# Linear attention on one core: query and key features over three PSUM banks, the next turn's first values product ahead of the state's update, the row transposes beside the key transposes, the scores in one run

## What is computed

```
B, S, D, H, DH = 4, 1024, 256, 16, 64          # all in float32
h = _ln(_layernorm(x), g1, beta1)
q = elu((h @ wq) per head @ proj) + 1
k = elu((h @ wk) per head @ proj) + 1
v = (h @ wv) per head
def step(carry, qkv_t):                         # over the S positions
    kv = kv + k_t[..., :, None] * v_t[..., None, :]
    ksum = ksum + k_t
    num = einsum('bhd,bhde->bhe', q_t, kv)
    den = einsum('bhd,bhd->bh', q_t, ksum) + 1e-06
    return (kv, ksum), num / den
attn = outs.reshape(b, s, H * DH) @ wo
x = normalised x + attn
```

## Time and profile before

| | us |
|---|---|
| median of 3 runs | 3779.68 (3776.72 to 3782.56) |
| the profiled execution, its own time | 3780.14 |
| its span, first to last instruction | 3778.3 |
| the stage of linear attention, about | 1214 to 2036 of the span |
| one turn of it, of 32 | 25.8 |
| TensorE busy, of the span | 3591.0 (95%) |
| mean granted TensorE clock | 0.989 |

### The profile page before, as it was taken

One profiled execution on the slowest core, in us unless ns is written; L12 is line 12 of the kernel. 1 busy time (PEld: TensorE's weight loads), 2 busy tenths in 40 slices (PEclk: granted clock), 3 DMA queues, 4 the chain that ended last, 5 costly groups with the idle time before them and its releaser, 6 DMA issues. The chain is left out here.

```text
span 3778.3 us, 59344 instructions
## 1 busy us (share of the span) xinstructions
PE 3591.0 (95%) x21704; PEld 2545.8 (67%) x21704; DVE 2510.6 (66%) x5351; ACT 1605.8 (42%) x3142; POOL 1403.5 (37%) x1569
## 2 busy tenths in 40 slices
PE   7889888887999999999999998999999999999999
PEld 5666666665556888888886665666656566666565
DVE  8999999997665555555554546777743367777432
ACT  5878777773001222222222214666631156666211
POOL 6988888885000000000001223444421134444111
PEclk9999999999999999999999999999999999999999
DMA  1000000002101000001001211111111111121121
GB/s 41 1 12 12 12 12 12 2 6 87 39 32 42 12 9 13 11 11 35 11 11 55 74 58 61 39 34 57 35 60 51 36 60 35 35 72 34 45 67 39
DMA packets 150758, 129.33 MB, mean 34 GB/s; under 512 B 20852, under 2 KB 147592, under 8 KB 150472
## 3 DMA queue, kind: packets, MB, share of 16 engines
q1 hardware_dynamic: 150472, 125.54, 10.7%
HBM read 87.73 MB, written 37.77 MB: 33 GB/s over the span
## 5 line engine op out<-in xcount | busy, mean ns | idle before, releaser
L420 POOL TENSOR_TENSOR ssm_acc<-ssm_acc,ssm_weighted 128x512 f32<-128x512 f32 x255 | 337.7, 1333 | 103.6 <-ACT ssm_weighted L565 103.0
L406 POOL TENSOR_SCALAR ssm_ub<-ssm_uT,ssm_bcT 128x512 f32<-128x512 f32 x512 | 357.5, 717 | 25.2 <-PE ssm_pu L1107 21.4
L1107 PEld LDWEIGHTS ssm_pu<-ident,ssm_ub 128*128 128x128 f32 x2048 | 239.6, 143 | 183.9 <-issue 87.5
L1107 PE MATMUL ssm_pu<-ident,ssm_ub 128*128 128x128 f32 x2048 | 310.2, 280 | 50.4 <-DVE ssm_state L780 33.1
L3074 PE MATMUL win_pa<-win_w_wqkv,tile_hT 128*128 128x512 f32 x744 | 342.7, 597 | 0.0
L1123 PE MATMUL ssm_pt<-ident,ssm_state 128*128 128x128 f32 x2040 | 278.8, 278 | 48.2 <-DVE ssm_acc L790 30.2
L2507 PE MATMUL glu_up<-block_hT,glu_w_w 128*128 128x512 f32 x704 | 310.0, 599 | 8.0 <-DVEq L82 8.0
L780 DVE TENSOR_TENSOR_SCAN ssm_state<-ssm_da,ssm_carry,ssm_pu 128x512 f32<-128x512 f32 x256 | 312.6, 1263 | 3.0 <-ACT ssm_da L553 3.0
L2845 POOL TENSOR_TENSOR block_hT<-tile_straight,tile_turned 128x512 f32<-128x512 f32 x124 | 157.9, 1274 | 401.9 <-DVE tile_turned L2952 401.7
L780 DVE TENSOR_TENSOR_SCAN ssm_state<-ssm_da,ssm_pu 128x512 f32<-128x512 f32 x256 | 297.0, 1202 | 5.4 <-PE ssm_pu L1107 2.7
L2889 ACT ACTIVATE win_probs<-win_sc,win_nbias,tile_rn 128x256 f32<-128x256 f32 x512 | 281.9, 560 | 28.7 <-DVE win_nbias L2980 21.8
(11 more groups left out here) (368 smaller groups left out, 7475.1 us busy)
## 6 DMA issues: line engine op xcount, KB each, us to landing
x<-block_y SPq DMA_DIRECT2D x16, 512.0 KB, 2.9
block_add<-x SPq DMA_DIRECT2D x16, 512.0 KB, 5.6
tile_raw<-in_tables SPq DMA_DIRECT2D x64, 128.0 KB, 2.2
a<-tile_y SPq DMA_DIRECT2D x64, 128.0 KB, 1.7
block_xs<-a SPq DMA_DIRECT2D x32, 256.0 KB, 3.3
block_x<-a SPq DMA_DIRECT2D x16, 512.0 KB, 5.2
x<-block_half_y SPq DMA_DIRECT2D x16, 256.0 KB, 2.1
block_x<-x SPq DMA_DIRECT2D x8, 512.0 KB, 3.9
```

Of the source, the lines that this page charges most:

```text
L406: nc.gpsimd.tensor_scalar(ub[:, i % 2, t, :], uT[:, k % 2, t, :], bcT[:, k % 2, t, n:n + 1], 1.0, ALU.mult, ALU.mult).then_inc(ub_ready.se ...
L420: nc.gpsimd.tensor_tensor(acc[:, k % 2, t, :], acc[:, k % 2, t, :], weighted[:, j, :], ALU.add)\
L1107: last = nc.tensor.transpose(pu[c][:, t * P:(t + 1) * P], ub[:, i % 2, t, c * P:(c + 1) * P], ident)
```

## The change

Four edits, all in `linear_attention_stage`; no product, copy or transfer is added or removed.

- The four groups of queries and keys go to `pa[0]`, `pa[1]`, `pc[2]`, `pa[0]` (`feature_banks`). Group 2 waits for the state's update of the turn before last instead of group 0's features, group 3 waits for group 0's features. In turn, the numerators' third bank `pc[2]` waits until VectorE has read group 2. The values go to `pa[1]` and `pa[0]` (`value_banks`), and wait for the features that read those.
- `values(turn.next(), 0)` stands between the numerators and the products for the state (L2069 in the changed file), not behind the latter.
- `transposes(turn.next())` stands right behind the key transposes, ahead of both halves of the scores, which so follow each other.
- On ScalarE the two `k_rows` copies stand ahead of the copy of `h`.

```diff
+        feature_banks, value_banks = [pa[0], pa[1], pc[2], pa[0]], [pa[1], pa[0]]
...
-                    nc.scalar.activation(grown[:, g % 2, :], pa[g % 2][:, :], ACT.Exp).then_inc(exp_ready.sem, 1)
+                    nc.scalar.activation(grown[:, g % 2, :], feature_banks[g][:, :], ACT.Exp).then_inc(exp_ready.sem, 1)
...
             def body(turn, before, more, more2):
 
+                act.wait_ge(keep_in.sems[turn.side], keep_in.at(turn))
+                for g in range(2):
+                    act.wait_ge(kt_ready.sem, kt_ready.at(turn.i, g + 1))
+
+                    nc.scalar.activation(
+                        k_rows[:, g * GP:(g + 1) * GP, :], pb[g][:, :].rearrange("p (r d) -> p r d", d=P), ACT.Copy,
+                        scale=keep[:, turn.side, :]).then_inc(k_rows_ready.sem, 1)
                 act.wait_ge(h_ready.sem, h_ready.at(turn.i))
                 act.wait_ge(y_ready.sem, y_ready.at(turn.i - 1))
                 nc.scalar.activation(h_keep[:, :], h[:, turn.side, :], ACT.Copy).then_inc(kept.sem, 1)
-                act.wait_ge(keep_in.sems[turn.side], keep_in.at(turn))
-                for g in range(2):
-                    act.wait_ge(kt_ready.sem, kt_ready.at(turn.i, g + 1))
...
                 for g in range(4):
                     if g < 2:
-                        pe.wait_ge(v_ready.sem, v_ready.at(turn.i - 1, g + 1))
+                        pe.wait_ge(v_ready.sem, v_ready.at(turn.i - 1, 2 - g))
+                    elif g == 2:
+                        pe.wait_ge(state_ready.sem, state_ready.at(turn.i - 2, 3))
                     else:
-                        pe.wait_ge(phi_ready.sem, phi_ready.at(turn.i, g - 1))
+                        pe.wait_ge(phi_ready.sem, phi_ready.at(turn.i, 1))
...
             def values(turn, g):
-                pe.wait_ge(phi_ready.sem, phi_ready.at(turn.i, 3 + g))
+                pe.wait_ge(phi_ready.sem, phi_ready.at(turn.i, 2 + 2 * g))
...
-                scores_of(turn, 1)
                 if more:
                     transposes(turn.next())
+                scores_of(turn, 1)
                 scores_of(turn, 0)
...
                     pe.wait_ge(state_ready.sem, state_ready.at(i - 1, c + 1))
+                    if c == 2 and more:
+                        pe.wait_ge(phi_ready.sem, phi_ready.at(i + 1, 3))
...
+                if more:
+                    values(turn.next(), 0)
                 pe.wait_ge(k_rows_ready.sem, k_rows_ready.at(i))
...
-                if more:
-                    values(turn.next(), 0)
                 pe.wait_ge(attn_ready.sem, attn_ready.at(i))
```

More of the change, by code:

```diff
@@ L1857, in values @@
                 nc.scalar.activation(v[:, turn.side, g * heads:(g + 1) * heads, 0:DH],
-                                                pa[g][:, :].rearrange("p (h d) -> p h d", d=DH), ACT.Copy).then_inc(v_ready.sem, 1)
+                                                value_banks[g][:, :].rearrange("p (h d) -> p h d", d=DH), ACT.Copy).then_inc(v_ready.sem, 1)
             def body(turn, before, more, more2):
-                act.wait_ge(h_ready.sem, h_ready.at(turn.i))
-                act.wait_ge(y_ready.sem, y_ready.at(turn.i - 1))
-                nc.scalar.activation(h_keep[:, :], h[:, turn.side, :], ACT.Copy).then_inc(kept.sem, 1)
                 act.wait_ge(keep_in.sems[turn.side], keep_in.at(turn))
@@ L1871, in body @@
                         scale=keep[:, turn.side, :]).then_inc(k_rows_ready.sem, 1)
+                act.wait_ge(h_ready.sem, h_ready.at(turn.i))
+                act.wait_ge(y_ready.sem, y_ready.at(turn.i - 1))
+                nc.scalar.activation(h_keep[:, :], h[:, turn.side, :], ACT.Copy).then_inc(kept.sem, 1)
                 if more:
@@ L1916, in features @@
                         qkT[:, turn.side, g // 2, g % 2 * GP:(g % 2 + 1) * GP, :],
-                        pa[g % 2][:, :].rearrange("p (r t) -> p r t", t=P), 0.0,
+                        feature_banks[g][:, :].rearrange("p (r t) -> p r t", t=P), 0.0,
                         grown[:, g % 2, :].rearrange("p (r t) -> p r t", t=P), ALU.max, ALU.add).then_inc(phi_ready.sem, 1)
@@ L1997, in queries_keys @@
                         for k in range(KD):
-                            last = nc.tensor.matmul(pa[g % 2][:, r * P:(r + 1) * P], wqk[:, g // 2, k, cols],
+                            last = nc.tensor.matmul(feature_banks[g][:, r * P:(r + 1) * P], wqk[:, g // 2, k, cols],
                                                     hT[:, k, :], start=(k == 0), stop=(k == KD - 1))
@@ L2002, in values @@
             def values(turn, g):
-                pe.wait_ge(phi_ready.sem, phi_ready.at(turn.i, 3 + g))
+                pe.wait_ge(phi_ready.sem, phi_ready.at(turn.i, 2 + 2 * g))
                 for k in range(KD):
-                    last = nc.tensor.matmul(pa[g][:, :], hT[:, k, :], wv[:, k, g * 512:(g + 1) * 512],
+                    last = nc.tensor.matmul(value_banks[g][:, :], hT[:, k, :], wv[:, k, g * 512:(g + 1) * 512],
                                             start=(k == 0), stop=(k == KD - 1))
```

## The result

| | before | after |
|---|---|---|
| median, us (4 runs each) | 3778.26 (3776.72 to 3782.56) | 3745.35 (3739.96 to 3746.80) |
| ratio, 95% interval | | 0.9908 (0.9891 to 0.9926) |
| the profiled execution, us | 3780.14 | 3739.96 |
| first key transpose of the stage, us of the span | 1214.47 | 1208.93 |
| that to the next stage's first product, us | 824.46 | 792.40 |

The forecast was 3745.6 for the median. "Before" has one run more here than in the table ahead of the prediction. The profiled execution of the changed kernel is the fastest of its four, and 40.2 us under that of before. Of these, 32.1 us lie in the stage; 5.5 us lie ahead of it, where the two programs are the same, and 2.6 behind it.

A forecast was written before the change was run, and what follows sets the result against it. TensorE was taken to bound the stage; 0.41 + 0.36 + 0.35 - 0.03 = 1.09 us a turn, 34.1 us in all, gave a median of 3745.6 us. Range 3739 to 3756, with 3739 to 3749 at 0.70.

The forecast's parts named there:

- scores in one run, copies of keys first: Head of a turn: one excursion into 64-row halves instead of two, and no late k_rows; 0.41 us a turn.
- residual as a wait: Row transposes, moved ahead, would wait for VectorE's residual to read pt; costs 0.03 us a turn, between 0 and 0.25.
- third bank: Queries and keys: group 2 no longer waits for group 0's features, so the weight loads run on; 0.36 us a turn.
- values ahead: Values product ahead of the state's products hides the wait for the division, 0.30, plus 0.05 from neighbours; 0.35 us a turn.
- The head: From the first key transpose to the first query product: 3.18 to 3.21 us instead of 3.59.
- the margin of 0.2 us for the copies: Both k_rows copies end near 1631.87; the second half of the scores wants pb at about 1632.17, weights 0.1 earlier.
- better neighbours: Values ahead: 64-column products left for transposes rather than 512-column products lose 0.05 instead of 0.10 us; 0.05 won.
- The entry into 64 columns: State's products behind a 512-column values product: the mode change costs 0 to 0.09 us, taken as 0.09; hidden gives 3742.7.
- Only the visible idle: Rival: only the idle shown returns, 0.69 us a turn, 21.4 us in all, giving 3758 us; chance of 3753 to 3761: 0.07.
- The residual in earnest: Rival: the residual wait costs 0.08 to 0.25 us a turn, 3747 to 3752.5 us; chance 0.16 together with k_rows still late.
- The third bank or the copies do nothing: Rival: another wait ends in the same place, say k_rows still late, 3752 us; chance 0.16 shared with the residual rival.
- Slower: Rival: the later state update outgrows its 4.2 us margin around the turn; 3789 us at 5.6 us longer; chance 0.04.

The follow-up runs named there:

- split: Changed kernel with the row transposes put back between the two halves of the scores, copies of the keys still first: 25.124 us a turn, median 3756.52 us.
- run with fourteen statistics: Changed kernel with fourteen extra, unused VectorE statistics of h ahead of n: 25.92 us a turn, one run of 3782.31 us.
- the two comparisons: Changed kernel against the kernel before, measured twice: 3745.35 against 3778.26 us (ratio 0.9908), then with no edit 3742.49 against 3777.33 us (0.9905).
- the first three: Changed kernel with one part undone each: third bank 3753.97 us, first values behind the state's products 3755.96, row transposes between the score halves 3756.52.

## Why the prediction was right, step by step

| per turn, us | forecast | in the changed kernel's starts | undone alone |
|---|---|---|---|
| scores in one run, copies of keys first | 0.41 | 0.38 | split 0.32; copies 0.38 |
| residual as a wait | -0.03 | 0 | |
| third bank | 0.36 | 0.35 | 0.352 |
| values ahead | 0.35 | 0.29 | 0.287 |
| sum | 1.09 | 1.02 | |

**The head.** Forecast 3.18 to 3.21 us, measured 3.20; the gain is 0.38 where I had 0.41. The missing 0.03 is the wait for `k_rows`. It didn't go, it shrank from 0.06 to 0.03. In the changed kernel the copies end at 1608.82 + 1.27 = 1610.09 and the weights of the second half of the scores start at 1610.20, the same 0.11 later as wherever they waited. No idle shows, since TensorE still runs the products of the first half, but the loads behind come late. The run with fourteen statistics shows the price, since its scores start after the copies are done:

```profile
1658.57 1.16 PE L2026 MATMUL lin_pc<-lin_space 64*128 64x128 f32 x16
1659.57 1.06 PE L2026 MATMUL lin_pb<-lin_space 64*128 64x128 f32 x16
1660.56 0.71 PE L2004 MATMUL lin_pa<-lin_hT,lin_wqk 128*128 128x128 f32 x4
```

From the first score to the first query it takes 1.99 us there and 1611.33 - 1609.31 = 2.02 in the changed kernel. What failed is the margin of 0.2 us for the copies. I let the first of them start the moment the fourth transpose ends, 0.60 after the first, and it starts 0.10 later; and I didn't take off the 0.11 from the end of a copy to the weights that wait for it, which I used for the residual. Together they eat the margin. So the second excursion was worth 0.35, as forecast, and the copies 0.03 instead of 0.06.

**The residual as a wait.** The weights of the row transposes start at 1608.92, 0.12 after the residual's end at 1608.80, so they are held for about 0.03 us, where I had 0.02. But the product doesn't need them yet: it starts at 1609.00, 0.11 after the last key transpose. That costs nothing where I had 0.03. So this error and that of the head cancel.

**The third bank.** Right: 0.352 against 0.36, with group 3's weights at 1616.68, 1.5 us after group 0's features (1615.20). Neither the numerators' third bank nor the values wait for the features.

**The values.** This term was mis-sized. The wait for the division was put at 0.30 and is 0.29. The 0.05 for better neighbours is zero. I had compared the run behind the state's products, 1.98 for the values against 1.88 (0.10) with 1.09 for the transposes against 1.04 (0.05). What I left out is that the values have a new neighbour too: behind the numerators' 65-column products their run takes 1.93, 0.05 longer than 1.88. The move spares 0.10 there and pays 0.05 twice. The entry into 64 columns behind a 512-column product was the unknown, between 0 and 0.09: its first product comes 0.52 after the last of the values (with 0.43 the step of those), so this cost is there in full. The other reading was that weight loads are pulled ahead of products in flight, as the Trainium skill, "TensorE: Matmul & The Clock Gate", part 2, says for row groups that don't conflict. This trace doesn't show it at this change of mode: the first weights of the state's products start at 1625.74, together with their own product.

**The sum.** A turn of 24.80 us lies outside the 24.7 to 24.75 that I named as a sign: 0.06 are missing at the values, and the two 0.03 cancel. The other signs came as said (row transposes 0.11 behind, no idle among the loads of queries and keys, 0.52 ahead of the state's products). Thirty turns at 1.02 are 30.7 us, where I had 32.7; the last one gave 0.30, as forecast, and turn 0 gave 0.92, where I had 1.1. Turn 0 depends on the clock too, which is 0.91 there in both traces (in the run with ScalarE's old order turn 0 takes 26.46 us at 0.94, in the changed kernel 27.13). With small change that makes 32.1 us, where I had 34.1. That the median came within 0.3 us of the forecast is partly luck: the base was 3779.7 then, and with more runs it is 3777 to 3779; and a launch scatters by more than the 2 us that the sum was off. By the medians of the two comparisons the gain is 32.9 and 34.8 us, each uncertain by some 6.

**The undone parts add up.** 0.352 + 0.287 + 0.320 + 0.06 for the copies in the old order is 1.02 us, the whole. The stage is 11.0, 8.9 and 9.5 us longer in the traces of the first three than in that of the changed kernel, where 31 turns give 10.9, 8.9 and 9.9. By launch times they lie 11.5, 13.5 and 14.0 us over the changed one's 3742.5 on that chip, up to 5 us more, while launches of the changed kernel alone lie up to 13 us apart.

**The rivals.** Only the visible idle: it would have given 21 us. 0.28 of 0.35 and 0.21 of 0.29 were visible in the waits; the 0.20 at `k_rows` was for the most part the change of mode, which leaves 0.17 idle without any wait for an engine (`lin_pc L2023` in the list after: 4.9 us in 29). The residual in earnest: there is 0.05 us to spare. The third bank or the copies do nothing: undone they cost 0.352 and 0.380, so both work, but the copies are in time only to within 0.03 us. Slower: excluded by 3.5 us of margin; I had it at 4.2, since I looked at `n` and the transposes that want it, and not at the residual, which stands behind `n` in VectorE's queue and is wanted half a microsecond earlier.

## What to carry to other kernels

On a TensorE that is busy all the time by its records, measure from start to start at each change of instruction. The idle time shown is no price: two waits cost a quarter to a third more than it (0.35 for 0.28, 0.29 for 0.21), the wait for `k_rows` cost 0.06 with 0.20 shown, and 0.03 with none shown; changes between tiling modes show no releaser at all. When a margin is a few tenths, take off the time from the end of one instruction to the start of the next engine's, here 0.06 to 0.11 at each hand-over. Put work of one mode in one run, and put a long product of other data between a result and the products that wait for its evacuation. Where a move on one engine brings work forward, see what then comes last, and move that in the same edit; one alone can measure as nothing.

## What of the hardware I had not expected

An excursion into halves of 64 rows and back costs 0.35 us here (0.09 + 0.10 on the way in, 0.10 + 0.05 out into transposes). One into halves of 64 columns costs some 0.29 (0.09 + 0.05 in, 0.09 + 0.05 out), read from starts alone, since no run leaves it out. Its entry adds 0.09 to the step even behind a 0.43 us product, so a long product doesn't cover it. Also without a change of mode, 512-column products behind 65-column ones lose 0.05 us once. And two engines that hang on the same product keep their distance: the weights of the row transposes follow the residual by 0.12 us in each of some 30 turns, with 0.05 us left before their product would be late, and that costs nothing.
